# A four-layer graph network on one core: node stages laid out anew (four banks for the typed sums, norms by statistics operations, first weight applied to the features)

## What is computed

```python
# layer 0 (the sums are linear, W1 can stand before or after them)
h = relu(segment_sum(norm[:, None] * (x @ W1)[src2], dst2) + b1)
h = relu(segment_sum(norm[:, None] * (h @ W2)[src2], dst2) + b2)
x = layernorm(x + h @ Wfc + bfc)
# layer 1
z = layernorm(x) * ln_gamma + ln_beta; xi = z @ W_in + b_in
...   # attention over edges
x = layernorm(x + agg @ W_ff + b_ff)
# layer 2: a weight for each of 8 node types, a mix of 4 basis matrices
...   # typed k, v, q, attention over edges
out = relu(decomp(agg, node_type, w_comp_a, w_basis_a) + x @ loop_weight + bias)
x = layernorm(x + out)
# layer 3
ht = x @ U_w.T + U_b; xw = x @ W_w.T + W_b
e = relu(ht[src] @ V1.T + ht[dst] @ V2.T + V_b) + ht[src] @ D_w.T + D_b + ht[dst] @ E_w.T + E_b
x = layernorm(x + segment_sum(xw[dst] * scaler * e, src))
```

## Time and profile before

| | us |
|---|---|
| time, median of 3 runs | 8421.61 (8416.38 to 8422.19) |
| profiled execution | 8421.25 |
| its span, first to last instruction | 8419.5 |
| PE, DVE, ACT, POOL busy | 5230.2, 4840.5, 3451.2, 4921.2 |
| four short stages | 1297.6 to 1356.5 |
| first node stage, first operation to that of the next stage | 2452.9 to 2535.0 |
| second (double-norm) node stage | 3645.4 to 3837.0 |
| stage with the typed k, v, q products | 5078.2 to 5465 |
| layer 3's node stage | 6797.3 to 7219.5 |
| last stage | 8314.8 to 8419.5 |

### The profile page before, as it was taken

How to read it: one execution, slowest core, us unless ns; L and a number is a source line. 1 busy time by engine, 2 the same in 40 slices (tenths; PEclk the granted TensorE clock), 3 DMA queues, 4 the chain that set the end, 5 groups by cost and what they waited for, 6 DMA issues and landing times. The chain is left out here.

```text
span 8419.5 us, 115306 instructions
## 1 busy us (share of the span) xinstructions
PE 5230.2 (62%) x25403; PEld 4100.3 (49%) x25404; DVE 4840.5 (57%) x14411; ACT 3451.2 (41%) x7679; POOL 4921.2 (58%) x4989
## 2 busy tenths in 40 slices
PE   6777773666655666653666657845555555567773
PEld 4555552444444444443666654334555433455552
DVE  7666664555545555563555554436666644566666
ACT  0222222444424444411656554435555421455552
POOL 0677775777747777725777740066666500577773
PEclk6665556888877888865656568967777667788886
DMA  1222221111222211123666653366666611566664
GB/s 40 56 51 49 51 44 53 50 51 50 51 33 59 50 50 51 50 20 102 178 170 177 176 129 105 129 192 203 203 203 200 167 33 41 177 205 204 206 204 108
DMA packets 808391, 920.90 MB, mean 109 GB/s; under 512 B 116546, under 2 KB 646474, under 8 KB 807818
## 3 DMA queue, kind: packets, MB, share of 16 engines
q0 software_dynamic: 198144, 441.54, 21.0%
q1 hardware_dynamic: 393738, 368.50, 14.8%
q10 hardware_dynamic: 216320, 109.07, 4.5%
HBM read 724.85 MB, written 193.87 MB: 109 GB/s over the span
## 5 line engine op out<-in xcount | busy, mean ns | idle before, releaser
L782 POOL DMA_INDIRECT arena<-t,stage_idx x3328 | 3257.6, 979 | 1444.9 <-issue 1021.3
L824 DVE TENSOR_TENSOR arena<-arena,ps 128x128 f32 (+2 forms) x4160 | 1299.0, 312 | 490.2 <-DVE arena L824 321.6
L1102 PE MATMUL ps<-arena 128*128 128x128 f32 x3328 | 659.6, 379 | 850.2 <-DMA arena<-t,stage_idx 850.2
L1565 PE MATMUL ps<-arena 128*128 x3328 | 639.4, 351 | 683.6 <-ACT arena L1467 661.2
L1102 PEld LDWEIGHTS ps<-arena 128*128 128x128 f32 x3328 | 612.1, 284 | 903.0 <-DMA arena<-t,stage_idx 467.7
L684 POOL DMA_INDIRECT d_rec<-arena x784 | 781.8, 997 | 448.2 <-issue 257.6
L2298 POOL DMA_INDIRECT arena<-t,stage_idx x832 | 811.4, 975 | 304.4 <-issue 239.1
L1565 PEld LDWEIGHTS ps<-arena 128*128 128x128 f32 x3328 | 609.5, 283 | 721.4 <-issue 721.3
L1591 PE MATMUL ps<-arena 128*128 128x136 f32 x3328 | 712.9, 392 | 357.6 <-DVEq L828 220.8
L1075 DVE TENSOR_SCALAR arena<-iota_row,stage_lw 128x128 f32<-128x128 f32 x1664 | 592.0, 361 | 595.2 <-PE ps L1102 595.1
L1591 PEld LDWEIGHTS ps<-arena 128*128 128x128 f32 x3328 | 649.7, 286 | 416.4 <-DVEq L828 258.1
(11 more groups left out here) (376 smaller groups left out, 9027.7 us busy)
## 6 DMA issues: line engine op xcount, KB each, us to landing
spill<-arena ACTq DMA_DIRECT2D x208, 512.0 KB
arena<-spill SPq DMA_DIRECT2D x208, 512.0 KB, 4.7
arena<-t,stage_idx POOLq DMA_INDIRECT x4160, 3.7
arena<-d_loT SPq DMA_DIRECT2D x208, 256.0 KB
arena<-s_loT SPq DMA_DIRECT2D x104, 512.0 KB, 4.5
arena<-key_d SPq DMA_DIRECT2D x98, 512.0 KB
t<-arena SPq DMA_DIRECT2D x98, 512.0 KB, 2.9
d_rec<-arena POOLq DMA_INDIRECT x784
```

Source lines behind the costliest of these rows:

```text
L782: pool.indirect_dma_start(out=rows[:, 8 * b + i, :], out_offset=None, in_=table, in_offset=bass.IndirectOffsetOnAxis(ap=stage_idx[:, 8 * b ...
L824: nc.vector.tensor_tensor(at, at, product, ALU.add).then_inc(self.added, 1)
L1102: last = nc.tensor.matmul(product(b, i), at[:, 8 * b + i, :], rows[:, 8 * b + i, :], start=True, stop=True)
L1565: last = nc.tensor.matmul(looked_up(b, z)[:, (i - 4 * z) * tab_w:(i - 4 * z + 1) * tab_w], hot_T[:, b, i * P:(i + 1) * P], tab[:, bass.ds( ...
```

## The change

- `Norm`: the sums are replaced by seven `bn_stats` (one tile each) and seven `bn_aggr`, which give mean and variance; the mean is subtracted after the signal to GpSimd. Used by all stages with a norm (their step counts follow).
- The four short stages become one. The table `t0` holds (x @ W1) * dinv: TensorE transposes and multiplies the features in seven pieces, three before and four after the fields of the records; each piece is stored by its own DMA.
- First node stage: no product any more; per tile one `scalar_tensor_tensor` (scale, bias) and one `tensor_scalar` (relu, scale), straight code, two buffers, a store for each group.
- Layer 3's node stage: typed products in four banks (4 to 7), wide rows in two (6 and 7); three typed products of the next group ahead of the transposes of the normed features, two behind them, two behind U; a wait for all sums of the group; then the seven wide products, W (its bias now added by VectorE), and the loop product of the next group. VectorE sums all typed products before the wide rows. ScalarE's first terms are moved likewise.
- Last stage: dp loaded in seven pieces, a scale and an add fused tile by tile, two buffers, the next group's sums between moments and scaling, straight code.

```diff
         class Norm:
...
-            def vector(self, step, r, sq, res, k, j):
-                m, v, inv_std = small[:, 0:GT], small[:, 16:16 + GT], small[:, 32:32 + GT]
-                step(nc.vector.tensor_reduce(m, r, AX.X, ALU.add))
-                step(nc.vector.tensor_scalar(m, m, -1.0 / D, None, ALU.mult))
-                step(nc.vector.tensor_tensor(r, r, bcast_last(m, D), ALU.add))
-                step(nc.vector.tensor_tensor(sq, r, r, ALU.mult))
-                step(nc.vector.tensor_reduce(v, sq, AX.X, ALU.add))
-                step(nc.vector.tensor_scalar(v, v, 1.0 / D, EPS, ALU.mult, ALU.add))
...
+            def moments(self, step, r):
+                for i in range(GT):
+                    one = nc.vector.bn_stats(self.parts[:, i, :], r[:, i, :])
+                step(one)
+                settle(nc.vector)
+                for i in range(GT):
+                    one = nc.vector.bn_aggr(self.stats[:, i, :], self.parts[:, i, :])
+                step(one)
+                step(nc.vector.tensor_scalar(small[:, 16:16 + GT], self.stats[:, :, 1], EPS, None, ALU.add))
                 step.eng.sem_inc(self.arg, 1)
+
+            def scale(self, step, r, res, k, j):
+                step(nc.vector.tensor_tensor(r, r, bcast_last(self.stats[:, :, 0], D), ALU.subtract))
                 step.eng.wait_ge(self.root, self.per * k + j + 1)
-                step(nc.vector.tensor_tensor(res, r, bcast_last(inv_std, D), ALU.mult))
+                step(nc.vector.tensor_tensor(res, r, bcast_last(small[:, 32:32 + GT], D), ALU.mult))
...
+                def features(k):
+                    need(pe, x_sb, k)
+                    transposes(x_cur[:, GC * k:GC * (k + 1)], 4).then_inc(x_up, 1)
+                    pe.wait_ge(x_sb, k + 1)
+                    need(pe, xw_rdy, k)
+                    products(x_T[k % 2], w["L0_gnn_W1"], 6).then_inc(xw_ps, 1)
...
+                for k in range(AHEAD):
+                    features(k)
+                pe.wait_ge(back, 32)
+                field(0, 1)
+                field(1, 0)
+                pe.wait_ge(v_back, 1)
+                field(2, 2)
+                pe.wait_ge(v_back, 4)
+                field(3, 3)
+                pe.wait_ge(v_back, 5)
...
+                for k in range(AHEAD, NG):
+                    features(k)
...
+                def products_out(k):
+                    dve.wait_ge(xw_ps, k + 1)
+                    nc.vector.tensor_tensor(cols(acc_gcn, k), tiled(pair(6)), bcast_last(dinv[:, GT * k:GT * k + GT], D), ALU.mult).then_inc(xw_rdy, 1)
...
+                for k in range(AHEAD):
+                    products_out(k)
+                dve.wait_ge(d_up, 1)
+                nc.vector.tensor_copy(keys_sorted, field_bank(0)).then_inc(v_back, 1)
+                dve.wait_ge(v_back, 1)
+                nc.vector.scalar_tensor_tensor(keys_sorted, d_tile_rep, -float(P), keys_sorted, ALU.mult, ALU.add).then_inc(v_back, 1)
+                dve.wait_ge(v_back, 2)
+                nc.vector.tensor_scalar(lo_sd, keys_sorted, float(P), None, ALU.min).then_inc(v_back, 1)
+                dve.wait_ge(d_up, 2)
+                nc.vector.tensor_copy(d_src[:, 0:SC], field_bank(1)).then_inc(v_back, 1)
...
+                products_out(AHEAD)
...
-                    step(nc.vector.tensor_tensor(tiled(A), cols(acc_gcn, k), bcast_last(dinv[:, bass.ds(GT * k, GT)], D), ALU.mult))
-                    dve.sem_inc(a_rdy, 1)
-                    dve.wait_ge(h_ps, k + 1)
-                    step(nc.vector.tensor_tensor(tiled(r), tiled(pair(2)), bcast_mid(bias["L0_gnn_b1"], GT), ALU.add))
-                    step(nc.vector.scalar_tensor_tensor(cols(acc_gcn, k), tiled(r), 0.0, bcast_last(dinv[:, bass.ds(GT * k, GT)], D), ALU.max, ALU.mult))
...
+                def sums_of(k):
+                    for i in range(GT):
+                        n = GT * k + i
+                        one = nc.vector.scalar_tensor_tensor(h[k % 2][:, i * D:(i + 1) * D], acc_gcn[:, n * D:(n + 1) * D], dinv[:, n:n + 1], bias["L0_gnn_b1"],
+                                                             ALU.mult, ALU.add)
+                    one.then_inc(n1_sum, 1)
...
+                def scaled_out(k):
+                    dve.wait_ge(n1_sum, k + 1)
+                    for i in range(GT):
+                        n = GT * k + i
+                        one = nc.vector.tensor_scalar(acc_gcn[:, n * D:(n + 1) * D], h[k % 2][:, i * D:(i + 1) * D], 0.0, dinv[:, n:n + 1], ALU.max, ALU.mult)
+                    one.then_inc(n1_out, 1)
+                sums_of(0)
+                for k in range(NG):
+                    if k + 1 < NG:
+                        need(dve, n1_out, k)
+                        sums_of(k + 1)
+                    scaled_out(k)
...
+                for k in range(NG):
+                    sp.wait_ge(n1_out, k + 1)
+                    sp.dma_start(table_rows(t1)[:, GT * k:GT * k + GT, :], cols(acc_gcn, k)).then_inc(n1_dma, 16)
...
+        def parts_bank(i):
+            return ps[:, (4 + i % 4) * 512:(5 + i % 4) * 512]
+
+        def rows_bank(i):
+            return bank(6 + i % 2)
...
+                    if more:
+                        for i in range(GT):
+                            for q in range(1, NB):
+                                sum_parts(k + 1, i, q)
...
+                    for i in range(GT):
+                        dve.wait_ge(vde_ps, GT * k + i + 1)
+                        step(nc.vector.tensor_tensor(rows5[:, i, 0:4 * D], rows_bank(i), vde_bias, ALU.add))
                     dve.wait_ge(w_ps, k + 1)
-                    y = rows5[:, :, 4 * D:R5]
-                    step(nc.vector.tensor_tensor(y, tiled(pair(0)), bcast_last(inv[:, bass.ds(GT * k, GT)], D), ALU.mult))
-                    for i in range(GT):
-                        if more:
-                            sum_parts(k + 1, i, 1)
-                        dve.wait_ge(vde_ps, GT * k + i + 1)
-                        step(nc.vector.tensor_tensor(rows5[:, i, 0:4 * D], ps[:, EXTRA:EXTRA + 512], vde_bias, ALU.add))
-                        if more:
-                            sum_parts(k + 1, i, 2)
-                            sum_parts(k + 1, i, 3)
-                    z = rows5[:, :, 3 * D:4 * D]
+                    y, z = rows5[:, :, 4 * D:R5], rows5[:, :, 3 * D:4 * D]
+                    step(nc.vector.tensor_tensor(y, tiled(pair(4)), bcast_mid(bias["L3_gnn_W_b"], GT), ALU.add))
+                    step(nc.vector.tensor_tensor(y, y, bcast_last(inv[:, bass.ds(GT * k, GT)], D), ALU.mult))
...
+                def typed(k, i):
+                    if i >= 4:
+                        pe.wait_ge(summed, SUMS * (GT * k + i - 3))
+                    nc.tensor.matmul(parts_bank(i), aT[:, i * P:(i + 1) * P], basis["a"], start=True, stop=True).then_inc(parts_ps, 1)
+
+                def loop(k):
                     pe.wait_ge(t_sb, 2 * k + 2)
-                    need(pe, v_n, LNS * k - LNS + 1)
                     products(x2T, w["L2_gnn_loop_weight"], 2, stop=False)
                     add_row("L2_gnn_bias", 2).then_inc(lp_ps, 1)
...
                     for i in range(GT):
                         typed(k, i)
+                    loop(k)
...
                 def turn(k, more):
                     if more:
                         start(k + 1)
-                    else:
-                        pe.wait_ge(v_r, ROWS_V * (k - 1) + 1)
+                        need(pe, v_r, ROWS_V * k)
+                        for i in range(EARLY):
+                            typed(k + 1, i)
+                        pe.wait_ge(t_sb, 2 * k + 4)
                     pe.wait_ge(x_rdy, k + 1)
                     transposes(x_new, 0).then_inc(xt_ps, 1)
+                    if more:
+                        for i in range(EARLY, 5):
+                            typed(k + 1, i)
                     pe.wait_ge(xt_sb, k + 1)
-                    products_T(U_T, x3T, 4).then_inc(h_ps, 1)
-                    products(x3T, W_T, 0, stop=False)
-                    add_row("L3_gnn_W_b", 0).then_inc(w_ps, 1)
+                    products_T(U_T, x3T, 0).then_inc(h_ps, 1)
+                    if more:
+                        for i in range(5, GT):
+                            typed(k + 1, i)
+                        pe.wait_ge(summed, SUMS * (GT * k + 2 * GT))
+                    else:
+                        pe.wait_ge(v_r, ROWS_V * k)
                     pe.wait_ge(h_sb, k + 1)
                     for i in range(GT):
-                        need(pe, v_r, ROWS_V * k + 1 + i if i else ROWS_V * k - 4)
-                        nc.tensor.matmul(ps[:, EXTRA:EXTRA + 512], hT[:, i * P:(i + 1) * P], VDE, start=True, stop=True).then_inc(vde_ps, 1)
-                        if more:
-                            typed(k + 1, i)
+                        if i >= 2:
+                            pe.wait_ge(v_r, ROWS_V * k + i - 1)
```

(35 more changed lines are left out.)

271 lines of the change are left out of this document (117 added, 154 removed).

## The result

| | us |
|---|---|
| kernel before, median of 4 runs | 8418.99 (8416.07 to 8422.19) |
| changed kernel, median of 4 runs | 8102.51 (8091.23 to 8107.69) |
| ratio, with its 95% interval | 0.9622 (0.9606 to 0.9639) |
| changed kernel, profiled execution | 8098.83, span 8097.1 |

The account below looks back on a forecast made before the run. The kernel was taken as bound by a chain of hand-overs, with no engine full. Terms of 51 + 9 + 25 + 11 + 117 + 33 = 246 us, taken from 8421, gave 8175 us, range 8125 to 8245.

Parts of the forecast that it names:

- Gather stages at no change: The five long gather stages, most of the 8419.5 us, are not edited and were taken at no change.
- Norm: Each norm on the path loses 2.45 us: 4.86 us before the signal to GpSimd become 2.4; 35 norms.
- Rival (a): Small operations cost their whole duration, so a norm gains 1.08 us less; whole kernel 8212 us; chance 15%.
- Layer 3's node stage: Largest term: -117 us (bounds -25 to -140), with turns of 40 us in place of 55.5.
- rival (c): TensorE stays at 1.2 GHz through the turns of layer 3's node stage; whole kernel 8270 us; chance 6%.
- Merged stage: Four short stages become one, with TensorE as its bound: -9 us (bounds -2 to -14).
- First node stage: Layer 0, without TensorE and ScalarE, stores group by group: 31.5 us in place of 82.1, -51 (-40 to -54).
- Double-norm stage: Second node stage: turns of 24.1 us become 20.8, with TensorE late next; -25 us (-15 to -34).
- Rival (b): GpSimd's power and VectorE's subtraction exclude each other, subtraction after power: +1.12 us on some 23 norms; 8201 us; chance 7%.
- (d): Better: 2.4 GHz throughout (18), double-norm turn 19.2 us (8), merged stage (5), quicker tensor_scalar (4): 8140 us; chance 11%.
- (e): Slower: bn_stats iterates like the reciprocal, 1.14 us each, +9.4 us on each of 35 norms; 8504 us; chance 2%.
- (f): The change does less than it says, such as a store or wait still holding the first node stage; 8225 us; chance 4%.

Follow-up runs that it names:

- e9: Changed kernel with three parts undone: no feature pieces ahead of the records' fields, first node stage's table in one store, dp in one load; 0.9738 of the kernel before.
- e4: Changed kernel with the older norm of the kernel before put back; 0.9779 of the kernel before.
- e7: Changed kernel with one idle one-element memset on VectorE between the signal to GpSimd and the subtraction of the mean; 0.9615 of the kernel before.

## Why the prediction was right or wrong

**What bounds it** was right: a chain of hand-overs, worth what is taken out of it.

**Gather stages at no change**: this step failed, and with it the range. The other unedited stretches held (conv stages within 3.5 us, layer 1's attention -5.0, the edge stage +7.7 in one profile and +0.6 in the next). Layer 2's attention gave 34.4 us, because an edit elsewhere moved VectorE's loop in the program. I had met the question once ("Straight code in place of the loop: no row prices its fetch") and asked it only of the edited stage. A row did price it: ten waits of 5.3 us, called "issue", at one loop's head, and ten more at L1684.

**Norm**: 2.45 us on the path. The operations' starts were right; that it fits to the hundredth is luck, 2.34 us to the signal for 2.41 and 1.72 from there to the scaling for 1.65. Rival (a) falls, 1.46 us a group and not 7 x 0.276.

**Layer 3's node stage**, mis-sized by 26 us. The turn against the forecast, in us behind its first operation:

| | forecast | measured |
|---|---|---|
| first transposes of TensorE | 4.8 | 4.7 |
| early typed products, start and end | 9.4, 14.6 | 9.0, 13.4 |
| last typed product ends | 21.7 | 19.1 |
| wide products start | 23.3 | 20.9 |
| W product ends | 32.4 | 29.6 |
| next turn | 40 | 37.4 |

The order of the steps and what each waits for came out as written; the middle one was too long, since I added up durations of TensorE's rows that overlap by 0.15 to 0.2 us at each change of group (the row of 4.40 us ends at 6746.91, behind the start of the next at 6746.74), and put the rise of the clock one product too late. Six turns of 37.0 for 40 make 18 us, with 5.5 in the last turn (38.7 us for 44) and 3 ahead of the first (18.1 for 21). The clock rose, so rival (c) falls.

**Merged stage**: right in kind ("TensorE becomes the stage's bound"), 8 us too cautious: from the second on a piece takes 3.6 us (second product 1.83 us, at 2.4 GHz already) where 5.5, 4 and 4.7 were forecast.

**First node stage**: 27.2 for 31.5. A group of seven takes 1.93 and 1.45 us, 3.34 together with the overlap (forecast 3.7 to 3.8, "0.19 if the latter are quicker": one starts every 0.20).

**Double-norm stage**: 30 for 25. The step that failed is "What is late next is TensorE", 20.7 us: from 3661.07 to 3680.16 a turn takes 19.1 us, VectorE's own sum (19.2). TensorE's last product takes 1.83 us for the 3.33 of the earlier trace rows and ends 15.7 us after the turn's first operation, and TensorE then stands idle for 2.83 us; the granted clock of the stage is 0.72 for 0.67. In the turn ahead of it, with two long powers, VectorE's turn took 21.0.

**Typed products' stage and last stage**: -12 and -32 for -11 and -33. e9 shows dp's pieces to be worth 6.6 us (forecast 5.5), e4 the norm 10.6.

**Rival (b)**, power and subtraction exclude each other: true, but mostly the other way round than priced. Against it stood that a power ran beside a VectorE operation; but that one had long started. In 8 of the 29 pairs that start together the power ends 0.95 us late (2.43 for 1.48) and the subtraction takes its 1.09; in the other 21 the power takes 1.48 and the subtraction 1.12 to 1.14. The Trainium skill (SBUF — State Buffer, SBUF: two separate sides) says that the one that starts first has the shared ports for its whole instruction. The 8 long powers agree with that if VectorE was first there, and I was too quick to set the lock aside; for the other side the trace doesn't agree, as I wrote: a VectorE operation that comes second waits 0.03 to 0.05 us, not the 1.48 of the power. All 8 together are 7.6 us (in e7 the double-norm stage fell by 5), not 26.

**Rivals (d), (e), (f)**: (d) names three of the four terms that came out, and with its 35 us still holds less than the edited stages gave; (e) and (f) fall.
